# State space stage: two of four channel tiles get their product with C on the turned state, by TensorE and ScalarE

## What is computed

```python
delta = softplus(dt_proj_w @ dt_lo + dt_proj_b)        # (batch, 512 channels, 512 tokens)
A = -exp(A_log)                                        # (512 channels, 16 states)
def step(state, xs):                                   # one token
    d_t, B_t, C_t, u_t = xs
    dA = exp(d_t[..., None] * A)
    state = state * dA + (d_t * u_t)[..., None] * B_t[:, None, :]
    y_t = einsum('ben,bn->be', state, C_t)
    return state, y_t
y = y + D * u
y = y * silu(z)
```

## Time and profile before

| | us |
|---|---|
| median of three runs | 4295.09 (4289.88 to 4296.61) |
| the profiled execution, its own time | 4301.73 |
| its span in the trace | 4299.9 |
| PE busy, share of the span | 4000.7, 93% |
| VectorE busy | 3105.3, 72% |
| ScalarE busy | 2296.8, 53% |
| first scan of the state space stage starts | 2812.5 |
| first product of the feed-forward part starts | 3560.6 |

### The profile page before, as it was taken

The page is one execution under the profiler, slowest core; times in us unless marked ns, Lnnn a source line. Parts: engine busy times, 40 slices in busy tenths (PEclk is TensorE's granted clock), DMA queues, the critical chain, the costliest instruction groups (busy, mean ns, idle before and its releaser), DMA issues. The chain is left out here.

```text
span 4299.9 us, 179869 instructions
## 1 busy us (share of the span) xinstructions
PE 4000.7 (93%) x76866; PEld 2486.6 (58%) x76866; DVE 3105.3 (72%) x5135; ACT 2296.8 (53%) x6321; POOL 933.6 (22%) x1927
## 2 busy tenths in 40 slices
PE   7999999999999999999999999757879789999998
PEld 4667767767676676767667676522333334444443
DVE  4788888888888888888888887478999991212221
ACT  4577776676676667676676766444344331111110
POOL 1333333333333333333233333100000000000000
PEclk8999999999999999999999999778989899999999
DMA  2222222222221212212122221142323332000000
GB/s 76 65 60 71 65 69 68 58 76 66 63 68 59 77 52 75 70 56 78 57 70 70 63 71 49 41 148 72 94 83 96 92 121 89 29 1 30 0 20 10
DMA packets 133721, 277.31 MB, mean 64 GB/s; under 512 B 21004, under 2 KB 62496, under 8 KB 129472
## 3 DMA queue, kind: packets, MB, share of 16 engines
q1 hardware_dynamic: 132784, 265.60, 20.2%
q10 hardware_dynamic: 144, 0.20, 0.0%
HBM read 235.07 MB, written 30.67 MB: 62 GB/s over the span
## 5 line engine op out<-in xcount | busy, mean ns | idle before, releaser
L420 PE MATMUL a_pb<-a_x_t,a_w_qkv 128*128 128x512 f32 x1536 | 844.0, 641 | 15.5 <-DMA a_x_t<-in_x_t 8.2
L1318 DVE TENSOR_TENSOR a_nq<-a_nq,a_tot 128x1024 f32<-128x1024 f32 x320 | 392.8, 1227 | 133.9 <-PE a_pb L451 85.2
L1281 DVE SCALAR_TENSOR_TENSOR a_acc<-a_pb,a_taps,a_acc 128x511 f32<-128x511 f32 (+2 forms) x576 | 425.5, 739 | 31.1 <-ACT a_acc L866 17.4
L2119 PE MATMUL m_p_y<-m_h,k_ident_sb 128*128 128x512 f32 x512 | 285.4, 710 | 130.7 <-DVE m_h L2356 130.7
L2830 DVE TENSOR_TENSOR a_x_t<-f_gate,f_pb 128x512 f32<-128x512 f32 x128 | 88.0, 687 | 383.1 <-ACT f_gate L2754 383.1
L2754 ACT ACTIVATE f_gate<-f_pb 128x512 f32<-128x512 f32 x132 | 78.8, 597 | 411.7 <-PE f_pb L2695 275.4
L420 PEld LDWEIGHTS a_pb<-a_x_t,a_w_qkv 128*128 128x128 f32 x1536 | 241.1, 192 | 99.0 <-issue 67.4
L451 PEld LDWEIGHTS a_pb<-a_nq,a_ks 128*32 128x32 f32 x20480 | 214.3, 111 | 143.3 <-issue 112.8
L2350 DVE TENSOR_TENSOR_SCAN m_h<-m_da,m_h 128x2048 f32<-128x2048 f32 x64 | 283.1, 4424 | 17.7 <-ACT m_da L2262 12.4
L1718 POOL COPY a_apt<-a_apt_fine 32x256 f32<-32x256 f32 x256 | 100.5, 393 | 882.4 <-DVE a_apt_fine L1336 857.8
L2119 PEld LDWEIGHTS m_p_y<-m_h,k_ident_sb 128*128 128x128 f32 x512 | 112.7, 228 | 295.1 <-DVE m_h L2356 161.9
(11 more groups left out here) (332 smaller groups left out, 8841.6 us busy)
## 6 DMA issues: line engine op xcount, KB each, us to landing
a_rows<-rows SPq DMA_DIRECT2D x192, 512.0 KB, 3.9
a_amp_sums<-amp_sums SPq DMA_DIRECT2D x64, 508.0 KB, 3.7
attn_o<-a_o_out SPq DMA_DIRECT2D x64, 256.0 KB, 2.7
m_b_rows<-ssm_bc SPq DMA_DIRECT2D x64, 256.0 KB, 3.7
m_c_rows<-ssm_bc SPq DMA_DIRECT2D x64, 256.0 KB, 4.5
k_big<-attn_o SPq DMA_DIRECT2D x16, 1024.0 KB, 8.3
a_w_qkv<-in_w_qkv SPq DMA_DIRECT2D x48, 256.0 KB, 3.2
k_big<-in_w_gu SPq DMA_DIRECT2D x3, 1536.0 KB, 13.3
```

The source lines that it names most:

```text
L420: mm = nc.tensor.matmul(pb[:, V_BANK if i == P_V else KQ_BANK], w_qkv[:, i, k], x_t[:, k, b * T:(b + 1) * T], start=(k == 0), stop=(k == D ...
L1281: last = nc.vector.scalar_tensor_tensor(acc[:, i, d:T], src[:, 0:T - d], taps[:, i, 3 - d:4 - d], acc[:, i, d:T], ALU.mult, ALU.add)
L1318: last = nc.vector.tensor_tensor(part, part, spread(blocks, list(part.shape)), ALU.mult)
L2119: nc.tensor.matmul(p_y[:, et], ident[:], h[:, (b * DS + n) % 3, et], start=(n == 0), stop=(n == DS - 1), skip_group_check=True).then_inc(s ...
```

## The change

SIDE = 2 tiles keep the way they had: `times_c` multiplies 1024 instead of 2048 columns and `sum_state` adds two tiles. The other TURNED = 2 tiles go another way. PE transposes the scanned tile (four 128x128 transposes into the new PSUM bank `p_h`, `turn_h`), so that tokens lie on the partitions; ScalarE copies each 128x128 block out of `p_h` with C of that state as one scale per partition into `h_turned_c` (`scale_h`); PE adds the result to `p_y`, in token order, with an identity (`sum_turned`). At a batch's end ScalarE copies the two turned tiles of `p_y` out (`keep_y`), PE turns them back (`turn_y`) and `finish` reads them. C per token (`c_token`) is made once a batch by four small transposes and a copy (`turn_c`, `keep_c`). `p_h` is one bank, so flip and scaling alternate. It takes a bank from `p_x`, which had two: the input projection and the dt products now use one, and the four dt products, formerly all at step 36 on PE and 40 on ScalarE, are spread over steps 36 to 43. ROWS goes from 3 to 2 for the broadcast rows, and SP issues a B row before it waits for the C product.

```diff
-        ROWS, LEAD = 3, 4
+        ROWS, LEAD = 2, 4
+        SIDE = 2
+        TURNED = ET - SIDE
...
-        PE_STEPS = {4 + 6 * et: et for et in range(ET)} | {31: DBL, 36: DT}
-        ACT_STEPS = {8 + 6 * et: et for et in range(ET)} | {30: U, 35: DBL, 40: DT, 43: SOFT_EXP, 46: SOFT_LOG}
+        PE_STEPS = {4 + 6 * et: et for et in range(ET)} | {31: DBL} | {36 + 2 * et: DT + et for et in range(ET)} | {47: C_TOKEN}
+        ACT_STEPS = ({8 + 6 * et: et for et in range(ET)} | {30: U, 35: DBL, 44: SOFT_EXP, 46: SOFT_LOG, 47: C_TOKEN}
+                     | {37 + 2 * et: DT + et for et in range(ET)})
...
                         if k >= ROWS:
+                            sp.wait_ge(dbu_ready, k - ROWS + 1)
+                        sp.dma_start(b_rows[:, k % ROWS], spread(io["ssm_bc"][b, n:n + 1], [P, T])).then_inc(b_in[k % ROWS], 16)
+                        if k >= ROWS:
                             sp.wait_ge(cs_ready, k - ROWS + 1)
-                        sp.dma_start(b_rows[:, k % ROWS], spread(io["ssm_bc"][b, n:n + 1], [P, T])).then_inc(b_in[k % ROWS], 16)
...
+                def turn_h(row, et):
+
+                    q = row * TURNED + et - SIDE
+                    pe.wait_ge(scanned, row + 1)
+                    if q:
+                        pe.wait_ge(h_scaled, q)
+                    pe.wait_ge(c_token_ready, tokens_before(row))
+                    for tt in range(TT):
+                        mm = nc.tensor.transpose(p_h[:, tt * P:(tt + 1) * P], h[:, row % 3, et, tt * P:(tt + 1) * P], ident[:])
+                    mm.then_inc(h_turned, 1)
+
+                def sum_turned(row, et):
+
+                    b, n = divmod(row, DS)
+                    if n == 0 and b:
+                        pe.wait_ge(y_ready, (b - 1) * ET + et + 1)
+                    pe.wait_ge(h_scaled, row * TURNED + et - SIDE + 1)
+                    nc.tensor.matmul(p_y[:, et], ident[:], h_turned_c[:, et - SIDE],
+                                     start=(n == 0), stop=(n == DS - 1), skip_group_check=True).then_inc(summed, 1)
...
                 for b in range(B):
                     for i in range(N):
-                        if i % ET == 1 and b * N + i > ET:
-                            for et in range(ET):
-                                sum_state(b * N + i - 1 - ET + et)
+                        if b and i == ET:
+                            for et in range(SIDE, ET):
+                                turn_y(b - 1, et)
+                        before_row = b * DS + i // ET - 1
+                        if before_row >= 0:
+                            if i % ET < TURNED:
+                                turn_h(before_row, SIDE + i % ET)
+                            if i % ET == 1:
+                                for et in range(SIDE):
+                                    sum_state(before_row * ET + et)
+                            if i % ET >= ET - TURNED:
+                                sum_turned(before_row, i % ET)
...
+                def scale_h(row, et):
+
+                    b, n = divmod(row, DS)
+                    act.wait_ge(h_turned, row * TURNED + et - SIDE + 1)
+                    act.wait_ge(c_token_ready, b + 1)
+                    if n == 0 and b:
+                        act.wait_ge(y_turned, (b - 1) * TURNED + et - SIDE + 1)
+                    elif row:
+                        act.wait_ge(summed, (row - 1) * ET + et + 1)
+                    for tt in range(TT):
+                        last = nc.scalar.activation(h_turned_c[:, et - SIDE, tt * P:(tt + 1) * P], p_h[:, tt * P:(tt + 1) * P],
+                                                    ACT.Copy, scale=c_token[:, b % 2, tt, n:n + 1])
+                    last.then_inc(h_scaled, 1)
...
                         if b * N + i + LEAD < B * N:
                             decay(b * N + i + LEAD)
+                        before_row = b * DS + i // ET - 1
+                        if before_row >= 0 and i % ET < TURNED:
+                            scale_h(before_row, SIDE + i % ET)
...
-                    nc.vector.tensor_tensor(h[:, row % 3], h[:, row % 3], spread(c_rows[:, row % ROWS:row % ROWS + 1], [P, ET, T]),
+                    nc.vector.tensor_tensor(h[:, row % 3, 0:SIDE], h[:, row % 3, 0:SIDE],
+                                            spread(c_rows[:, row % ROWS:row % ROWS + 1], [P, SIDE, T]),
                                             ALU.mult).then_inc(cs_ready, 1)
```

126 lines of the change are left out of this document (95 added, 31 removed).

## The result

The changed kernel takes 4377.32 us (median, 4375.37 to 4382.23) against 4295.85 (4289.88 to 4296.72): ratio 1.0198, 95% interval 1.0183 to 1.0214, +81.5 us. The forecast was 4333 with a range to 4373: the sign was right, the size less than half. The profiled execution after took 4375.37 us, 73.6 more than that of before, 4301.73.

What follows compares the result with a forecast made beforehand. VectorE was taken to set the pace, with slack on PE and ScalarE. First to fourth batch and tail, 4.0 + 14.1 + 12.4 + 3.9 + 3.6 = +38 us, made 4333 us from 4295; range 4262 to 4373.

Steps and rivals of the forecast that it cites:

- Rules 1 to 3: Scan and flip times: VectorE's 7.84 us a row plus other work, PE's program order, ScalarE's decays behind scalings.
- W: PE's work per row up to its last flip: 4.32 us, 0.86 more per projection, plus preparation.
- rule 3: ScalarE: the scan two rows on ends at least 7.2 us after F, its last decays standing behind the scaling.
- rule 2: PE: F is W after the later of the previous row's F and 1.2 us past the scan's end.
- F: End of PE's flip of a row's fourth tile; 14.1 us forecast for row 0 of the second batch.
- the walk: Row-by-row forecast of the second batch: 38.6 us of waits on 156 of VectorE need, 194 against 179.9 us.
- E: End of a row's scan on VectorE, counted in the second batch from the end of its first scan.
- Rival (c): PE's clock drops to half speed where PE idles: some 10 us a batch, 4373 us in all; chance 0.14.
- Between the two flips PE waits for ScalarE: Within a row, PE waits at least 1.67 us for the scaling, covered by two projections or not.
- Costed at nothing: the two rows of B and C.: Two broadcast rows instead of three: no cost in the sum; product with B late by up to 2 us.
- (a): Slack absorbs the added work, VectorE stays the bound: 4230 us, chance 0.11; partial form 4240 to 4286, chance 0.14.
- (b): Nothing measurable, within 0.2% or 8.6 us of 4295, new waits some 60% of those counted; chance 0.06.

Runs made afterwards that it cites:

- warmed: Changed kernel with products that nobody reads put into PE's queue ahead of its longest waits; ratio 1.0176 to the kernel before, recurrence 818.6 us.
- the structure alone: Changed kernel with nothing turned (SIDE = 4), keeping two broadcast rows, one p_x bank and spread dt products; ratio 1.0060 to the kernel before, recurrence 767.2 us.

## Why the prediction was right in sign and short in size

**What bounds it, and what is removed.** Right: 68.2 us went from VectorE, forecast 68.5, and came back as waits.

**Durations of what is added.** Right or a little high. A set of four flips took its slot for 0.44 us, as taken from the earlier trace rows; a set of four scalings 1.14 us against 1.27. PE after, second batch:

```profile
3125.79 0.60 PE L2096 MATMUL m_p_h<-k_ident_sb,m_h 128*128 128x128 f32 x4
3126.23 1.88 PE L2189 MATMUL m_p_y<-m_h,k_ident_sb 128*128 128x512 f32 x4
```

The Trainium skill's factor of four for transposes (TensorE: Matmul & The Clock Gate, Terms) gives an estimate of 0.22, and the row is against it here. PE was busy 167.8 us in the second batch, against 142 by need at full clock.

**Rules 1 to 3.** Right in kind. Three runs act on one rule each and answer in its direction: flips ahead of PE's other work (W) -47, decays further ahead (rule 3) -33, taps ahead of the scaling -20. They share one path, so they don't add.

**The step that failed: rule 2, the end of the flips F, which was worked out with PE at full clock.** Rule 3 is right: with the measured F and the constants of the walk it gives the scans it was made for. Second batch of the changed kernel, us from the end of the first scan; "rule 2" is the rule with the measured scan and flip before it:

```
row of the flip               0      5      7      8      9     10     14
F forecast                 14.1   75.2  105.2  116.9  127.4  138.6  181.4
F by rule 2                14.1   78.4  110.9  125.7  136.3  148.6  193.6
F measured                 16.9   81.2  114.0  125.8  137.4  149.0  195.6
F measured, warmed         14.3   75.8  107.1  118.8  130.4  142.0  188.3
scan that waits               2      7      9     10     11     12     16
E by rule 3, F measured    24.1   95.8  121.7  134.3  146.4  160.7  208.2
E measured                 23.8   95.5  121.4  133.8  145.9  162.0  208.1
```

Rule 3 is off by 0.5 us at most, but for row 12 (1.3). Rule 2 is short by 2.8, 2.8 and 3.1 us in rows 0, 5 and 7, 1.1 in row 9 and 2.0 in row 14. With the 1.3 of row 12 that is 13 of the batch's missing 14.1 us. In the first three of these rows the two plain sums took twice their time, and in row 9 nearly so, beside row 0 (3013.51 above):

```profile
3081.19 3.78 PE L2189 MATMUL m_p_y<-m_h,k_ident_sb 128*128 128x512 f32 x4 [3.21 <-DVE m_h L2480]
...
3109.04 3.78 PE L2189 MATMUL m_p_y<-m_h,k_ident_sb 128*128 128x512 f32 x4 [6.89 <-DVE m_h L2480]
...
3137.97 3.37 PE L2189 MATMUL m_p_y<-m_h,k_ident_sb 128*128 128x512 f32 x4
```

(1) *The clock was put down as a rival to the forecast and not as a term of it.* Rival (c) had a price of about 10 us a batch, and rows 12 to 15, the start of the next batch and row 7 as its places; the waits that the forecast itself put on PE's path are what stands in front of the slow sums (2.81, 3.21 and 6.89 us in the rows shown; only 1.71 us in front of that in row 9). By the table it makes up to 9.8 us of the second batch, in rows 0, 5, 7 and 9. Runs show 7.3 and 6.4 us of it in the second and third batch, 7 to 13 in all; the added products stand in front of some waits only (eight slow sets in the second batch became three), and in none of the last batch. With them, the flips of rows 0 and 5 come within 0.2 and 0.6 us of the forecast. (2) *"Between the two flips PE waits for ScalarE"*, put at 1.67 us. In row 14 the two flips start 3.5 us apart, because ScalarE has norm_1 between the two scalings: 2.0 us, the same in the warmed kernel. ScalarE after:

```profile
3202.20 2.93 ACT L2321 ACTIVATE m_x<-m_sums,m_stats 128x512 f32<-128x512 f32 x4
3205.03 0.72 ACT L2375 ACTIVATE m_da<-a_x_t,m_neg_a 128x511 f32<-128x511 f32 x1
3205.64 1.12 ACT L2303 ACTIVATE m_h_turned_c<-m_p_h,m_c_token 128x128 f32<-128x128 f32 x4
```

(3) *"Costed at nothing: the two rows of B and C."* In steady rows that was right, but the third row is no longer loaded ahead: 5 us at the start. (4) *Rows 10 and 11* are 3.3 us longer than forecast, unchanged by the added products. Of this 1.1 is the late flip of row 9 in the table and 1.3 the Exp, which stands in front of a scaling in row 11; the dt products are waited for there too. The walk left these terms out. ScalarE after, in row 11:

```profile
3156.84 0.69 ACT L2277 ACTIVATE a_x_t<-m_p_x,m_cols 128x512 f32<-128x512 f32 x1 [3.06 <-PE m_p_x L2073]
...
3159.19 1.14 ACT L2303 ACTIVATE m_h_turned_c<-m_p_h,m_c_token 128x128 f32<-128x128 f32 x4 [0.48 <-PE m_p_h L2096]
3160.42 1.91 ACT L2283 ACTIVATE a_x_t<-a_x_t 128x2048 f32<-128x2048 f32 x1
```

But with those steps moved, row 11 took 13.9 us, as forecast, and row 9 15.2 instead of 12.4, so they are a shift of the same wait and no separate cause.

Of the missing 46 us, 5 (rows), 7 to 13 (clock) and at most 3 (dt steps) are shown by runs. The other 25 to 31 are some 3 in the first batch and 6 to 8 in each other. In the second batch the table places most of them, by reading a trace and not by a run: what the added products left of the clock, norm_1 and the Exp. The third batch has the same spacings within 0.3 us a row. For the first and the last batch the prediction gives no walk row by row to hold against the trace, and their part, some 9 us, stays open. The 19 us of the structure alone cannot be counted as their cause, since most of them vanish under the flips.

**Rivals.** (a) fell by the result: by duration PE and ScalarE had the slack, and the recurrence became 84 us longer. How long it would be with no link left between the two engines is not shown; the run that cut one of two links gave 765.9 us against 748.1. (b), no measurable difference, fell too. (c) was real, but as an addition. That 4377 lies 4 us from its price of 4373 is luck: the price was for 40 us of clock, of which runs show 7 to 13.

## What to carry to other kernels

Before moving work from the pacing engine to two with slack, write down for each engine what stands between the producer's end and the new consumer in its program order. Need by duration said 68 us faster here; the order said slower, and it was the order that could be changed for 47 us by moving the flips of a row ahead in TensorE's loop. When a run is to cut a link, list every semaphore between the two engines: here one was cut, and the wait moved to the next. When a forecast puts new waits on TensorE's path, its clock belongs in the sum, row by row, and not among the rivals. When runs of single parts are priced with the main part taken out, check the price with it in: the dt steps cost 11 us without the flips and 3 with them.

## What the runs showed of the hardware

Plain sums ran at 1.2 GHz (granted clock 0.50) behind two waits of 4.11 and 2.81 us with only flips between; a wait of 3.27 us behind products and one set of flips did not lower the clock (1.00). A 128x128 scaling out of PSUM by one value per partition took 1.14 us for four, less than the 1.27 of four from SBUF. VectorE's products of 1024, 1536 and 2048 columns took 1207, 1740 and 2273 ns on average: 1.04 ns a column and 141 ns besides.
